# A recurrence on one Trainium2 core: the weights stand in TensorE and the state passes, instead of the other way round

## The chip, the cores and the metric

The kernel is one program on one core of one Trainium2 chip. TensorE (PE in the profile, its loads of the standing operand PEld) multiplies; VectorE (DVE), ScalarE (ACT) and GpSimd (POOL) work elementwise; SyncE (SP) issues most of the transfers. The engines run side by side and wait for each other with semaphores. A matmul has a standing operand, which is loaded first, and a moving one, which passes through it; its result goes to PSUM (`ps`, 8 banks of 512 f32 in each of 128 partitions). The metric is the time of one execution on the device in microseconds, less is better.

## The reference

The whole is one transformer-like block: a recurrence, a long convolution over its states, a gated scan, a shared MLP and a mixture of 16 experts. The change is in the first part alone:

```python
xw = jnp.einsum('ntd,dh->nth', x, Wx) + b          # x: 8 x 512 x 256

def step(prev_h, xw_t):
    next_h = jnp.tanh(xw_t + prev_h @ Wh)          # prev_h: 8 x 256, Wh: 256 x 256
    return (next_h, next_h)
_, hs = jax.lax.scan(step, h0, jnp.swapaxes(xw, 0, 1))
```

The 512 steps can't be done side by side: each needs the state of the one before, for all 8 sequences. All operands are f32. The convolution behind it needs the kernel K, a sum of exponentials of each channel, and all states.

## The kernel before

Constants: P = 128, B = 8 sequences, D = 256, C = 2 (halves of 128 channels), Q = 32, J = 4, W = 64, G = 8 steps in a group, IT = 32 loop turns of 16 steps (two groups, `bank` 0 and 1). J counts four column positions of TensorE's array (`tile_position=(0, Q * j)`): a matmul with at most 32 standing columns can sit in each, and its result lands in partitions 32j to 32j+31.

The state of a step is standing (128 channels x 8 sequences, twice, for the halves k), the weights `wh` move: for each half and each position j one matmul of 8 x 64 (L521). The result has sequences in partitions and 64 channels along a row, so after tanh (L859, into `zt`, two halves of 32 columns) it has to be turned: VectorE transposes blocks of 32 x 32 (L1139, `turn`) into `hring`, a ring of 16 states in `tok`, from which the next step's matmuls load. In PSUM the four banks 0 to 3 hold the sums, two banks for each group.

While a step's state is on its way through ScalarE and VectorE, TensorE adds the input of the same step of the next group to its PSUM area (`xpart`, L500, 8 matmuls with `xst` standing and `wx` moving) and the bias (L503, 4 matmuls of one row, 1 x 8 standing). In steps 11 to 14 of a turn it also does `kernel_sums` (L490), a piece of the convolution's kernel, whose arguments POOL makes once a turn (L399) and ScalarE turns into exponentials in steps 2 to 9 (L863). POOL copies each finished group of states to `uT` (L420, `keep`), and `s_hist` tells that the ring's half may be written again. VectorE builds `cblk` (L1123) in step 4 and takes the finished piece out of PSUM (L1128, L1130) in step 15; SP stores it to `k_pad`.

SP's queue is in order: the first loads (`first`, `state`, nine small `loads`, among them `rows_to` last), then in each turn an `xst` load for each group (`ahead`, waits for `s_xdone`), and beside it either `x_tok` and `slots_in` (turns 0 to 15), or the convolution's matrices into `ring` (turns 17 to 28), and the store of the piece. ScalarE's four exponentials at the start (L847 to L850) and `lam` (L852) stand ahead of its first tanh and wait for all nine loads. `keep_up` is a matmul of zeros over the whole array; eight of 512 columns stand at the program's start.

## Time and profile before

| | us |
|---|---|
| time of the runs, median of 3 | 1144.24 (1143.5 to 1145.04) |
| the profiled execution, its span | 1136.0 |
| PE busy | 1042.3 (92%) |
| PEld busy | 782.3 (69%) |
| DVE busy | 580.7 (51%) |
| ACT busy | 547.1 (48%) |
| POOL busy | 311.8 (27%) |

```text
span 1136.0 us, 62532 instructions
## 1 busy us (share of the span) xinstructions
PE 1042.3 (92%) x26280; PEld 782.3 (69%) x26280; DVE 580.7 (51%) x1954; ACT 547.1 (48%) x1956; POOL 311.8 (27%) x308
## 2 busy tenths in 40 slices
PE   8899999999999999997798999999998999999994
PEld 5566666666666666666685444457888999999994
DVE  2333333333333333336585898998754655645641
ACT  2333333333333333337685777673344665665652
POOL 2111111111011111012240005437602455455455
PEclk7999999999999999999899999999999999999998
DMA  2121221122433333203861001104325566566644
GB/s 86 50 75 63 74 75 63 60 74 66 47 42 41 42 41 44 28 10 58 184 133 41 1 0 62 46 32 145 141 66 177 127 148 156 124 148 149 131 61 47
DMA packets 85349, 89.63 MB, mean 79 GB/s; under 512 B 8657, under 2 KB 71654, under 8 KB 85298
## 3 DMA queue, kind: packets, MB, share of 16 engines
q1 hardware_dynamic: 70706, 71.87, 25.2%
q0 software_dynamic: 14592, 17.10, 9.0%
q8 instruction: 31, 0.51, 0.2%
q14 instruction: 20, 0.16, 0.1%
HBM read 56.82 MB, written 33.96 MB: 80 GB/s over the span
## 4 chain that ended last, share of the span: by engine, by line
PE 64%; DVE 11%; ACT 9%; issue 7%; POOL 5%; DMA 2%; SPq 1%; POOLq 1%; DVEq 0%; ACTq 0%
PE ps L521 18%; PE ps L793 14%; PE ps L807 7%; DVE tok L1139 7%; PE ps L659 7%; ACT zt L859 6%; PE ps L500 4%; PE ps L503 3%; PE ps L709 2%; PE ps L490 2%; POOL slots_in L446 2%; PE ps L581 2%; PE ps L566 2%; PE ps L718 2%; POOL big L420 1%
## 5 line engine op out<-in xcount | busy, mean ns | idle before, releaser
L1139 DVE STREAM_TRANSPOSE tok<-zt 128x32 f32<-128x32 f32 x1024 | 159.6, 194 | 331.3 <-ACT zt L859 310.7
L859 ACT ACTIVATE zt<-ps 128x32 f32<-128x32 f32 x1024 | 146.2, 195 | 332.3 <-PE ps L521 332.3
L521 PE MATMUL ps<-wh,tok 128*8 128x64 f32 x8192 | 212.1, 222 | 43.4 <-DVE tok L1139 1.9
L500 PE MATMUL ps<-wx,xst 128*8 128x64 f32 x8320 | 217.7, 221 | 1.1 <-issue 1.1
L521 PEld LDWEIGHTS ps<-wh,tok 128*8 128x8 f32 x8192 | 118.1, 88 | 123.9 <-DVE tok L1139 110.3
L465 POOL DMA_INDIRECT out<-arena,dest x80 | 127.6, 1595 | 98.8 <-ACT arena L1017 79.6
L503 PE MATMUL ps<-brow,tri 1*8 1x64 f32 x4160 | 153.9, 217 | 0.7 <-issue 0.7
L500 PEld LDWEIGHTS ps<-wx,xst 128*8 128x8 f32 x8320 | 145.0, 91 | 4.7 <-issue 2.4
L793 PE MATMUL ps<-xgT_hi,ew_hi 128*128 128x320 f32 (+1 forms) x384 | 118.7, 309 | 4.1 <-DVE spare L1281 1.6
L793 PE MATMUL ps<-xgT_hi,ew_lo 128*128 128x320 f32 (+1 forms) x384 | 119.0, 310 | 0.0
L793 PE MATMUL ps<-xgT_lo,ew_hi 128*128 128x320 f32 (+1 forms) x384 | 118.2, 308 | 0.0
L1387 DVE TENSOR_TENSOR mid<-mid,ps 128x320 f32<-128x320 f32 (+1 forms) x96 | 46.7, 486 | 106.4 <-ACT mid L1035 104.4
L503 PEld LDWEIGHTS ps<-brow,tri 1*8 1x8 f32 x4160 | 58.2, 82 | 59.9 <-issue 2.9
L420 POOL TENSOR_TENSOR big<-tok,zero 128x128 f32 x64 | 29.1, 455 | 231.8 <-DVE tok L1139 231.8
L399 POOL TENSOR_TENSOR arena<-dta_q,iota_t 128x512 f32<-128x512 f32 x33 | 34.3, 1039 | 208.4 <-PE ps L490 207.3
L659 PE MATMUL ps<-mid,gw 128*128 128x512 f32 x192 | 85.3, 602 | 2.4 <-ACT mid L945 1.6
L446 POOL DMA_INDIRECT slots_in<-tok,arena x64 | 75.5, 1179 | 23.6 <-issue 17.1
L1035 ACT ACTIVATE mid<-ps 128x320 f32<-128x320 f32 (+1 forms) x96 | 41.9, 436 | 72.2 <-PE ps L793 72.2
L793 PEld LDWEIGHTS ps<-xgT_hi,ew_hi 128*128 128x128 f32 (+1 forms) x384 | 68.7, 179 | 4.9 <-DVE spare L1281 1.9
L807 PE MATMUL ps<-ew_hi,eact_hi 128*128 128x256 f32 (+1 forms) x240 | 71.7, 299 | 0.3 <-ACT arena L1017 0.3
L659 PEld LDWEIGHTS ps<-mid,gw 128*128 128x128 f32 x192 | 36.7, 194 | 47.4 <-issue 46.1
L793 PEld LDWEIGHTS ps<-xgT_lo,ew_hi 128*128 128x128 f32 (+1 forms) x384 | 68.8, 179 | 0.0
(206 smaller groups left out, 1754.6 us busy)
## 6 DMA issues: line engine op xcount, KB each, us to landing
ring<-k_pad SPq DMA_DIRECT2D x64, 256.0 KB, 6.2
slots_in<-mid SPq DMA_DIRECT2D x16, 645.0 KB, 3.3
mid<-slots_in SPq DMA_DIRECT2D x16, 645.0 KB, 4.2
arena<-in_ex_down SPq DMA_DIRECT2D x16, 384.0 KB, 3.2
arena<-in_ex_gate SPq DMA_DIRECT2D x16, 352.0 KB, 4.7
arena<-in_ex_up SPq DMA_DIRECT2D x16, 352.0 KB, 5.9
xst<-in_x_steps SPq DMA_DIRECT2D x66, 64.0 KB, 1.8
xtok<-in_x_tok SPq DMA_DIRECT2D x16, 256.0 KB, 2.7
```

Of the source, the lines that this page charges most:

```text
L446: pool.indirect_dma_start(out=slots_in[:, :], out_offset=bass.IndirectOffsetOnAxis(ap=idx[:, k, r:r + 1], axis=0), in_=hid_tok[:, r, :], i ...
L465: pool.indirect_dma_start(out=out[:, :], out_offset=bass.IndirectOffsetOnAxis(ap=dest[:, z, t:t + 1], axis=0), in_=yo[:, z, t], in_offset= ...
L500: nc.tensor.matmul(sums_at(bank, t)[Q * j:Q * j + B], xst[:, bank, k, t], wx[:, k, j * W:(j + 1) * W], start=t < 2 and k == 0, stop=False, ...
L503: last = nc.tensor.matmul(sums_at(bank, t)[Q * j:Q * j + B], tri[0:1, 1, 0:B], brow[:, j * W:(j + 1) * W], start=False, stop=False, skip_g ...
L521: last = nc.tensor.matmul(sums_at(bank, t)[Q * j:Q * j + B], hring[:, (n - 1) % (2 * G), k, 0:B], wh[:, k, j * W:(j + 1) * W], start=False ...
L659: last = nc.tensor.matmul(ps[:, gate_bank(n % NT, q), :], gw[:, q, c, z * P:(z + 1) * P], x1T[:, c, 4 * b:4 * b + 4, :].rearrange("p r t - ...
L793: last = nc.tensor.matmul(ps[0:fw, 2 * h + m % 2, 0:HALF], of(w)[:, c, f0:f0 + fw], v[:, c, hf * HALF:(hf + 1) * HALF], start=c == 0 and p ...
L807: last = nc.tensor.matmul(ps[:, 4 + (z + t) % 2, 0:D], a[0:fw, f, t * P:(t + 1) * P], down_of(w)[0:fw, f], start=f == 0 and p == 0, stop=f ...
L859: nc.scalar.activation(zt[:, n % 2, half], sums_at(n // G, n % G)[:, half], ACT.Tanh).then_inc(s_zt, 1)
L1035: nc.scalar.activation(esil[0:fw, m % 2], ps[0:fw, m % 2, 0:HALF], ACT.Silu).then_inc(s_esil, 1)
L1139: nc.vector.transpose(hring[:, n, k], zt[:, n % 2, k * Q:(k + 1) * Q]).then_inc(s_h, 1)
L1387: nc.vector.tensor_tensor(eprod[0:fw, m % 2], esil[0:fw, m % 2], ps[0:fw, 2 + m % 2, 0:HALF], ALU.mult).then_inc(s_eact, 1)
```

## The change

- `wh` is standing now (128 x 32 columns, L531 of the new file) and the state moves (8 columns). A step has 16 matmuls: for each half o of the result and each half k of the state one for each position j. The result has channels in partitions and sequences along the row, as the next step wants it, so ScalarE writes tanh (128 x 8, L875) straight into `hring`; `zt`, `s_zt` and VectorE's `turn` are gone. `hring` has 8 columns for a state's half instead of 32.
- Half 0 and half 1 of the result lie in different banks (`sums_at(bank, t, o)`), half 0 is complete after 8 of the 16 matmuls (`s_sum[0]`), half 1 after 16. There is a semaphore of its own for each half, on both sides. The wait for `s_hist` moves from VectorE to ScalarE.
- The input is no longer added step by step: `inputs_summed` does it for 8 steps at once, 64 columns moving. A group takes six calls, in its steps t = 1 to 6: for each half o the bias (`brow` standing, one row of 32 columns, and a row of ones moving), then the two halves of `wx`. 24 matmuls a group in place of 96.
- In all steps but 11 to 14 `keep_up(256)` stands behind the rest.
- The nine small loads move from SP's to ScalarE's queue, ahead of its table load; `tri` goes from the first loads to the late ones.
- VectorE's loop holds `kernel_states` and `kernel_out` alone.

On TensorE, in the loop before, from the second wait of step 0 to the start of step 1 (`tok` is the ring of states, `wh` and `wx` the weights, `xst` the inputs):

```order
L521 MATMUL ps<-wh,tok 8x64 [waits s_h]
L521 MATMUL ps<-wh,tok 8x64 x3
L525 ISA
L500 MATMUL ps<-wx,xst 8x64 [waits s_xs1]
L500 MATMUL ps<-wx,xst 8x64 x7
L503 MATMUL ps<-brow,tri 8x64 x4
```

On TensorE, in the loop now, from the end of step 1 to the end of step 2 (`spare` holds the ones, `zero` the zeros of keep_up):

```order
L510 MATMUL ps<-spare,brow 32x64 x4
L489 MATMUL ps<-zero 128x256
L529 REGISTER_ALU
L531 MATMUL ps<-tok,wh 32x8 [waits s_h0]
L531 MATMUL ps<-tok,wh 32x8 x3
L531 MATMUL ps<-tok,wh 32x8 [waits s_h1]
L531 MATMUL ps<-tok,wh 32x8 x11
L535 REGISTER_ALU
L510 MATMUL ps<-xst,wx 32x64 [waits s_xs1]
L510 MATMUL ps<-xst,wx 32x64 x3
```

Eight products a step became 16 with other operands standing, twelve of them behind the second wait, and the 12 products of input and bias became 4 in six steps of eight, with keep_up behind.

On ScalarE, from the program's start to the first step, before:

```order
L845 ACT_TABLE_LOAD
L847 ACTIVATE a_bc<-a_bc 128x64 [waits s_const]
L848 ACTIVATE a_q<-a_q 128x2
L849 ACTIVATE dt_bc<-dt_bc 128x256
L850 ACTIVATE dt_q<-dt_q 128x66
L852 ACTIVATE lam<-dta_q 128x128 [waits s_dta]
L866 UNCONDITIONAL_BRANCH
L866 ISA
L859 ACTIVATE zt<-ps 128x32 [waits s_sum]
L859 ACTIVATE zt<-ps 128x32
```

And now, from the last but one of its nine loads:

```order
L859 DMA iota_t<-in_iota_t 128x128
L859 DMA rows_to<-in_rows_to 128x37
L860 ACT_TABLE_LOAD
L862 ACTIVATE a_bc<-a_bc 128x64 [waits s_const]
L863 ACTIVATE a_q<-a_q 128x2
L864 ACTIVATE dt_bc<-dt_bc 128x256
L865 ACTIVATE dt_q<-dt_q 128x66
L867 ACTIVATE lam<-dta_q 128x128 [waits s_dta]
L882 UNCONDITIONAL_BRANCH
L882 ISA
L874 ISA [waits s_hist]
L875 ACTIVATE tok<-ps 128x8 [waits s_sum0]
```

The nine loads stand ahead of the table load, and a tanh waits for its half alone.

The diff, cut to its core:

```diff
...
         xst = sb("xst", [P, 2, C, G, B])
-        zt = sb("zt", [P, 2, W])
+        ones = spare[0:1, 0:G * B]
         shared = ExitStack()
...
         tok = shared.enter_context(nc.sbuf_tensor("tok", [P, R * DX], F32))
         u_tok = tok[:, 0:R * D].rearrange("p (g j r) -> p g j r", j=J, r=R)
         hid_tok = tok[:, :].rearrange("p (r d) -> p r d", d=DX)
-        hring = tok[:, 7168:7168 + 2 * G * C * Q].rearrange("p (n k q) -> p n k q", n=2 * G, k=C)
+        hring = tok[:, 7168:7168 + 2 * G * C * B].rearrange("p (n k b) -> p n k b", n=2 * G, k=C)
         mid = shared.enter_context(nc.sbuf_tensor("mid", [P, R * D], F32))
         x1T = mid[:, :].rearrange("p (c r t) -> p c r t", c=C, t=P)
         blank = mid[:, 0:CT * DX].rearrange("p (t d) -> p t d", t=CT)
...
         s_kst = sem("s_kst")
         s_state = sem("s_state")
         s_late = sem("s_late")
+        s_sum = [sem("s_sum0"), sem("s_sum1")]
+        s_h = [sem("s_h0"), sem("s_h1")]
         s_tile = [sem("s_tile%d" % n) for n in range(NSLOT)]
         s_yst = [sem("s_yst0"), sem("s_yst1")]
         s_ewg = [sem("s_ewg0"), sem("s_ewg1")]
...
         s_xg = [sem("s_xg0"), sem("s_xg1")]
         block = ctx.enter_context(nc.Block())
-        first = ((wx, wx_d), (tri, tri_d), (brow, b_rec_d))
+        first = ((wx, wx_d), (brow, b_rec_d))
         state = ((wh, wh_d), (h0r, h0_rec))
         loads = ((a_q, a_q_d), (dt_q, dt_q_d), (a_bc, a_bc_d),
                  (dt_bc, dt_bc_d), (c_q, c_q_d), (d_k, d_k_d), (consts, consts_d), (iota_t, iota_t_d), (rows_to, rows_to_d))
-        late = ((ident, ident_d), (h0g, h0_gate), (gw, gate_w), (gb, gate_b), (rw, router_w), (rb, router_b),
+        late = ((ident, ident_d), (tri, tri_d), (h0g, h0_gate), (gw, gate_w), (gb, gate_b), (rw, router_w), (rb, router_b),
                 (resets, resets_d), (iota_e, iota_e_d))
         FIRST_LOADED, STATE_LOADED, LOADED, LATE = 16 * len(first), 16 * len(state), 16 * len(loads), 16 * len(late)
         NT = 2 * C
+        NIN = C * (C + 1)
         def gate_bank(t, q):
             return (2 * t) % 6 + q if q < 2 else 2 + t
...
                 return ((0, 1), (4, 5), (4, 5))[nf % 3]
             return nf % 2, 2 + nf % 2
-        def sums_at(group, t):
-
-            return ps[:, 2 * group + t % 2, t // 2 * W:(t // 2 + 1) * W]
+        def sums_at(bank, t, o):
+
+            return ps[:, 2 * bank + o, B * t:B * t + B]
+
+        def columns(j, o):
+
+            return slice(W * j + Q * o, W * j + Q * o + Q)
         def u_out(engine, copy, half, done):
...
             for dst, src in state:
                 sp.dma_start(dst[:], src).then_inc(s_state, 16)
             sp.dma_start(xst[:, 1], x_steps[1]).then_inc(s_xs[1], 16)
-            for dst, src in loads:
-                sp.dma_start(dst[:], src).then_inc(s_const, 16)
             sp.wait_ge(s_zero, 1)
             sp.dma_start(k_pad[:, 0:P].rearrange("(c p) t -> p c t", p=P), zero[:, 0:C * P].rearrange("p (c t) -> p c t", c=C)).then_inc(s_kst, 16)
...
             def keep(i, half):
-                group = hring[:, G * half:G * half + G, :, 0:B][:, ::-1].rearrange("p t k b -> p k t b")
+                group = hring[:, G * half:G * half + G][:, ::-1].rearrange("p t k b -> p k t b")
                 pool.wait_ge(s_zero, 1)
-                pool.wait_ge(s_h, 4 * G * i + 2 * G * half + 2 * G + 2)
+                pool.wait_ge(s_h[0], 2 * G * i + G * half + G + 1)
+                pool.wait_ge(s_h[1], 2 * G * i + G * half + G + 1)
                 pool.tensor_tensor(uT[:, :, bass.ds(i * (-2 * G) + (S - G - G * half), G), :], group, zeros, ALU.add).then_inc(s_hist, 1)
             with pool.Fori(0, IT) as i:
                 keep(i, 0)
...
                     last.then_inc(s_kmm, 1)
-            def xpart(bank, t):
-
-                for k in range(C):
-                    for j in range(J):
-                        nc.tensor.matmul(sums_at(bank, t)[Q * j:Q * j + B], xst[:, bank, k, t], wx[:, k, j * W:(j + 1) * W],
-                                         start=t < 2 and k == 0, stop=False, skip_group_check=True, tile_position=(0, Q * j))
+            def inputs_summed(bank, n):
+
+                o, c = n // (C + 1), n % (C + 1) - 1
                 for j in range(J):
-                    last = nc.tensor.matmul(sums_at(bank, t)[Q * j:Q * j + B], tri[0:1, 1, 0:B], brow[:, j * W:(j + 1) * W],
-                                            start=False, stop=False, skip_group_check=True, tile_position=(0, Q * j))
+                    if c < 0:
+                        w, v = brow[0:1, columns(j, o)], ones
+                    else:
+                        w, v = wx[:, c, columns(j, o)], xst[:, bank, c].rearrange("p t b -> p (t b)")
+                    last = nc.tensor.matmul(ps[Q * j:Q * j + Q, 2 * bank + o, 0:G * B], w, v, start=c < 0, stop=c == C - 1,
+                                            skip_group_check=True, tile_position=(0, Q * j))
                 return last
+
             for _ in range(WARM):
                 keep_up(512)
             pe.wait_ge(s_ps0, 1)
             pe.wait_ge(s_first, FIRST_LOADED)
             pe.wait_ge(s_xs[0], 16)
-            for t in range(G):
-                last = xpart(0, t)
+            for n in range(NIN):
+                last = inputs_summed(0, n)
             last.then_inc(s_xdone, 1)
             def steps(i, bank):
                 for t in range(G):
                     n = bank * G + t
-                    for k in range(C):
-                        pe.wait_ge(s_h, 4 * G * i + 2 * n + k + 1)
-                        for j in range(J):
-                            last = nc.tensor.matmul(sums_at(bank, t)[Q * j:Q * j + B], hring[:, (n - 1) % (2 * G), k, 0:B], wh[:, k, j * W:(j + 1) * W],
-                                                    start=False, stop=True, skip_group_check=True, tile_position=(0, Q * j))
-                    last.then_inc(s_sum, 1)
-                    if t == 0:
+                    for o in range(C):
+                        for k in range(C):
+                            if o == 0:
+                                pe.wait_ge(s_h[k], 2 * G * i + n + 1)
+                            for j in range(J):
+                                last = nc.tensor.matmul(sums_at(bank, t, o)[Q * j:Q * j + Q], wh[:, k, columns(j, o)], hring[:, (n - 1) % (2 * G), k],
+                                                        start=False, stop=k == C - 1, skip_group_check=True, tile_position=(0, Q * j))
+                        last.then_inc(s_sum[o], 1)
+                    if t == 2:
                         pe.wait_ge(s_xs[1 - bank], 16 * i + 16 + 16 * bank)
-                    last = xpart(1 - bank, t)
-                    if t == G - 1:
-                        last.then_inc(s_xdone, 1)
+                    if 1 <= t <= NIN:
+                        last = inputs_summed(1 - bank, t - 1)
+                        if t == NIN:
+                            last.then_inc(s_xdone, 1)
+                    if not 11 <= n < 11 + 2 * NH:
+                        keep_up(256)
                     if 11 <= n < 11 + 2 * NH:
                         if n == 11:
                             pe.wait_ge(s_ps0, 1)
...
         @block.scalar
         def _(act):
+            for dst, src in loads:
+                act.dma_start(dst[:], src).then_inc(s_const, 16)
             act.preload_act_table(ACT.Tanh)
             act.wait_ge(s_const, LOADED)
             nc.scalar.activation(a_bc[:], a_bc[:], ACT.Exp).then_inc(s_dtm, 1)
...
             def steps(i):
                 for n in range(2 * G):
-                    act.wait_ge(s_sum, 2 * G * i + n + 1)
-                    for k in range(C):
-                        half = slice(k * Q, (k + 1) * Q)
-                        nc.scalar.activation(zt[:, n % 2, half], sums_at(n // G, n % G)[:, half], ACT.Tanh).then_inc(s_zt, 1)
+                    if n % G == 0:
+                        act.wait_ge(s_hist, 2 * i + n // G + 1)
+                    for o in range(C):
+                        act.wait_ge(s_sum[o], 2 * G * i + n + 1)
+                        nc.scalar.activation(hring[:, n, o], sums_at(n // G, n % G, o), ACT.Tanh).then_inc(s_h[o], 1)
                     if 2 <= n < 2 + KG * NH:
                         if n == 2:
                             act.wait_ge(s_kq, i + 1)
...
                 chain[0] = chain[0] + 1
                 dve.wait_ge(s_c, chain[0])
+            nc.vector.memset(ones, 1.0)
             nc.vector.memset(ps[:, 0:5], 0.0).then_inc(s_ps0, 1)
             nc.vector.memset(xc[:], 0.0).then_inc(s_hist, 2)
             nc.vector.memset(ctmp, 0.0).then_inc(s_x1, 2)
+
             dve.wait_ge(s_state, STATE_LOADED)
-            nc.vector.tensor_copy(hring[:, 2 * G - 1, :, 0:B], h0r[:]).then_inc(s_h, 2)
+            for k in range(C):
+                nc.vector.tensor_copy(hring[:, 2 * G - 1, k], h0r[:, k]).then_inc(s_h[k], 1)
             dve.wait_ge(s_const, LOADED)
             dve.wait_ge(s_dtm, 4)
             nc.vector.tensor_tensor(dta_q[:], dt_q[:].unsqueeze(2).to_broadcast([P, NG + KG, NH]), a_q[:].unsqueeze(1).to_broadcast([P, NG + KG, NH]), ALU.mult).then_inc(s_dta, 1)
...
-            def turn(i, n):
-                if n % G == 0:
-                    dve.wait_ge(s_hist, 2 * i + n // G + 1)
-                for k in range(C):
-                    dve.wait_ge(s_zt, 4 * G * i + 2 * n + k + 1)
-                    nc.vector.transpose(hring[:, n, k], zt[:, n % 2, k * Q:(k + 1) * Q]).then_inc(s_h, 1)
-            def steps(i):
-                for n in range(2 * G):
-                    turn(i, n)
-                    if n == 4:
-                        kernel_states(i)
-                    if n == 15:
-                        kernel_out(i)
             with dve.Fori(0, IT) as i:
-                steps(i)
+                kernel_states(i)
+                kernel_out(i)
             u_out(dve, lambda to, v: nc.vector.tensor_copy(to, v), 0, s_uev)
```

## Rows read from the trace of the kernel before

**Rows 1.** Timeline, ScalarE's first and last tanh: start us, length us, engine, line.

```profile
11.97 0.27 ACT L859 ACTIVATE zt<-ps 128x32 f32<-128x32 f32 x2
...
515.40 0.29 ACT L859 ACTIVATE zt<-ps 128x32 f32<-128x32 f32 x2 [0.69 <-PE ps L521]
```

**Rows 2.** The page's costliest groups: busy us, mean ns | idle before, releaser.

```profile
L1139 DVE STREAM_TRANSPOSE tok<-zt 128x32 f32<-128x32 f32 x1024 | 159.6, 194 | 331.3 <-ACT zt L859 310.7
L859 ACT ACTIVATE zt<-ps 128x32 f32<-128x32 f32 x1024 | 146.2, 195 | 332.3 <-PE ps L521 332.3
...
L521 PEld LDWEIGHTS ps<-wh,tok 128*8 128x8 f32 x8192 | 118.1, 88 | 123.9 <-DVE tok L1139 110.3
```

**Rows 3.** Timeline of one steady step.

```profile
300.70 0.41 PE L521 MATMUL ps<-wh,tok 128*8 128x64 f32 x16
...
300.93 0.41 PE L500 MATMUL ps<-wx,xst 128*8 128x64 f32 x16
301.18 0.28 ACT L859 ACTIVATE zt<-ps 128x32 f32<-128x32 f32 x2 [0.49 <-PE ps L521]
...
301.26 0.29 PE L503 MATMUL ps<-brow,tri 1*8 1x64 f32 x8
...
301.41 0.31 DVE L1139 STREAM_TRANSPOSE tok<-zt 128x32 f32<-128x32 f32 x2 [0.66 <-ACT zt L859]
...
301.67 0.41 PE L521 MATMUL ps<-wh,tok 128*8 128x64 f32 x16
```

**Rows 4.** Timeline of TensorE in the convolution: 32 columns standing.

```profile
554.22 0.30 PE L569 MATMUL ps<-arena 128*32 128x64 f32 x8
554.33 0.41 PE L566 MATMUL ps<-ring,arena 128*32 128x128 f32 x8
```

**Rows 5.** Groups by form, loads of 32 columns: 553 to 556, then 547.9 to 551.4.

```profile
L569 PEld LDWEIGHTS ps<-arena 128*32 128x32 f32 x32 | 1.0, 110 | 0.0
...
L569 PEld LDWEIGHTS ps<-arena 128*32 128x32 f32 x32 | 1.6, 177 | 0.1
```

**Rows 6.** Timeline of TensorE where the array's division changes.

```profile
5.90 0.29 PE L503 MATMUL ps<-brow,tri 1*8 1x64 f32 x8
6.12 0.41 PE L500 MATMUL ps<-wx,xst 128*8 128x64 f32 x16
...
538.85 0.66 PE L590 MATMUL ps<-ident,arena 128*128 128x128 f32 x4
539.43 0.42 PE L566 MATMUL ps<-ring,arena 128*32 128x128 f32 x8
```

**Rows 7.** Timeline of the start.

```profile
0.74 1.28 ACT L845 ACT_TABLE_LOAD   x1 [0.74 <-PEq L1497]
...
7.65 1.44 SPq L294 DMA_DIRECT2D rows_to<-in_rows_to  x1
...
10.52 0.26 ACT L847 ACTIVATE a_bc<-a_bc 128x64 f32<-128x64 f32 x1 [8.50 <-DMA rows_to<-in_rows_to]
```

**Rows 8.** The page's transfers: number, KB each, us to landing.

```profile
ring<-k_pad SPq DMA_DIRECT2D x64, 256.0 KB, 6.2
```

**Rows 9.** Windows: from:to, us, busy of PE, PEld, DVE, ACT, POOL, granted clock, DMA, GB/s.

```profile
8.64:12.05 3.41, 1.93 (x84) 1.10 (x72) 0.29 (x1) 1.10 (x7) 0.43 (x2) 1.00 0.20 49
18.88:22.29 3.41, 3.41 (x112) 2.16 (x107) 0.93 (x6) 1.05 (x7) 0.00 (x0) 0.50 0.02 5
100.00:500.00 400.00, 365.67 (x16856) 242.81 (x16856) 138.72 (x898) 137.28 (x924) 48.52 (x77) 1.00 0.26 52
541.11:544.53 3.42, 1.06 (x38) 0.80 (x30) 2.20 (x8) 1.98 (x4) 1.24 (x1) 1.00 0.83 181
544.53:547.94 3.41, 2.53 (x29) 2.00 (x30) 0.00 (x0) 0.58 (x3) 0.71 (x1) 0.50 0.91 194
```

**Rows 10.** Timeline of one step at half the clock.

```profile
17.07 0.61 PE L521 MATMUL ps<-wh,tok 128*8 128x64 f32 x16
...
17.46 0.65 PE L500 MATMUL ps<-wx,xst 128*8 128x64 f32 x16
17.75 0.29 ACT L859 ACTIVATE zt<-ps 128x32 f32<-128x32 f32 x2 [1.53 <-PE ps L521]
...
18.04 0.40 PE L503 MATMUL ps<-brow,tri 1*8 1x64 f32 x8
```

4 lines of the change are left out of this document (2 added, 2 removed).

## The prediction

> [...]
>
> (1) *The price p of such a set.* The trace has no product with 8 columns moving. Upper bound: products with 32 columns standing and 64 moving go at 0.11 us per 8, so 0.056 per set [rows 4], and fewer moving columns can't take longer. Lower bound: a load. One of 32 columns shows 110 ns [rows 5], one of 8 columns 88 in the same clock [rows 2]: 22 ns for 24 columns, 0.9 ns each, so 32 columns occupy a position for 28 ns or so, and the next load for that position can't begin before the product ahead has taken up its weights. With 64 columns moving that hides; with 8 (an eighth of the 53 ns that 0.057 leaves after some issue, 7 ns) it is the load that counts. I take p = 0.030, nearest to the load row, and keep 0.028 to 0.057.
>
> (2) *The chain of one step.* Half 0 is summed first, but half 0 of the next step needs both halves of the state too, so the chain goes through half 1: its tanh, then the 6 sets from the second wait on. First to last product: first load 0.027, five sets of 0.030, 0.02 of stagger: 0.197. From the last product to tanh: today 0.48 less the 0.194 from first to last start is 0.286, less 0.047 for 56 columns fewer: 0.24. Tanh to TensorE: 0.23 today from tanh to a waiting engine, of which 0.195 is the instruction; 24 columns fewer may save 0.01; the hop into TensorE is 0.05, where the hop into VectorE is 0.03: 0.235. Sum **0.67 us** a step against 0.97. The transposes, 0.26 a step, are gone, and nothing replaces them.
>
> (3) *TensorE's own time in a step.* Here the cover is thin. The one-row bias product and keep_up(256) use another division of the array than the sums. What a change of division costs is in the trace: 16 instructions before the one-row product take 0.33 instead of 4 x 0.057 [rows 3], and 8 one-row instructions take 0.22 instead of 0.11 until the next can start [rows 6]; four whole-array products of 128 columns (0.107 each at 2.4 GHz, 0.43, and about 0.05 for the first load) are followed only 0.58 after the first start [rows 6]. So 0.10 to 0.11 each. Whole-array work of 256 bf16 columns streams 0.107 at 2.4 GHz, with 0.015 for its load (bounds 0 and 0.055).
> - Steps without input (4 of 16): sums 0.267 (0.027 + 8 x 0.03), change 0.105, keep_up 0.122, change 0.105: 0.60, under the chain's 0.67.
> - Steps with a wx set pair (0.114): 0.71. Five of 16.
> - Steps with a bias pair: one change more, 0.82. Three of 16.
> - Steps with kernel_sums in place of keep_up (4 of 16): three 0.67 by the chain; the one with a bias 0.73.
>
> Sum for 16 steps: 7 x 0.67 + 5 x 0.71 + 3 x 0.82 + 0.73 = 11.43, 0.714 a step. 511 of them are 365 us; a loop turn costs 0.07 more than its steps today (0.985 against 0.97, mostly), 2 us in all.
>
> (4) *Loads on ScalarE's queue.* rows_to is issued at 7.65 and the first activation stands at 10.52, tanh at 11.97 [rows 7]. Nine issues of 0.48 from 0.74 put rows_to at 4.6, and the table load of 1.28, now behind them, still ends by 7.5. Gain 3 us; nothing if the first activation waits for another transfer. TensorE has 12 sets of input to do instead of 80 before the first step; it is hidden either way.
>
> (5) *What hides.* A ring load takes 5.7 to 6.2 us to land [rows 8] and two go in each loop turn, now 11.5 us long, not 15.6; xst has 12 steps (8.6 us) between its release and its use. POOL's copy and arguments (0.46 and 1.04 us) have half a turn, 5.7 us. VectorE keeps three small operations per turn. All at nothing; if an xst load came late behind the ring, up to 2 us in each of 12 turns, 24 us, which is in the range.
>
> (6) *The clock.* It is at 1.2 GHz from 12.05 to 25.7 today, after TensorE stood still before 12.45 (1.93 of 3.41 us busy) [rows 9]. After the change TensorE stands still from about 6.3 to 9, so I expect a slow start here too, of about the same 13 us, at 0.2 to 0.4 us a step: 3 to 6 us, 3 taken.
>
> Sum: 503.4 - 365 - 2 - 3 + 3 = 136 us less. Span 1000, time **1008 us**.
>
> **Where a rule speaks against it.** Sixteen products start within 0.23 us, 14 ns apart [rows 3], because the four positions run side by side. The Trainium skill, "TensorE: Matmul & The Clock Gate", Part 1, "Wait — 56ns, not 53.3ns?", says that start to start never drops below about 25 ns however small the product; the row disagrees for products in different positions, and an estimate by that rule (32 x 0.025 a step, plus 0.45 of the rest) would be 1.25 us a step, slower than today. The measurement decides.
>
> **The rivals.**
> *A. A small product costs as much as one of 64 columns* (p = 0.057, the upper bound of (1)). The chain becomes 0.81, sums 0.483, the kinds of step 0.82, 0.93, 1.03, 0.81 and 0.95; mean 0.90; 460 us. Saved 43 - 2 + 3 - 3 = 41: **1103 us**. For it: no row shows less than 0.056 per set. Against: what fills that set is its 64 columns. Beside it: the Trainium skill, "TensorEngine Tiling (Array Packing)", "Instruction Overhead", says that a product of one column has the latency of one with 60; by that rule it is this rival. Chance 0.12.
>
> *B. Half clock throughout, loads lengthened with it: slower.* The place is the same stage. At 1.2 GHz a load of 32 columns shows 177 ns, not 110 [rows 5]: p = 0.057. The step before shows the rest of the prices at that clock [rows 10]: sets of 64 columns 0.10 to 0.107 (0.39 for the first four), a change of division 0.15 (0.58 for 16 instructions less four sets), first product to tanh 0.68, of which 0.30 lies between the first and the last start. Chain 0.38 - 0.09 (56 columns fewer) + 0.33 (six sets) + 0.24 = 0.86; sums 0.48 + change 0.15 + keep_up 0.23 + change 0.15 = 1.02; with a wx pair 1.23; with a bias 1.38; kernel steps 0.91 and 1.24. Mean 1.146, 586 us, with the loop turns and the loads of (3) and (4) 82 more than now: **1226 us**. keep_up itself does harm there, since TensorE is then the bound in every step. It decides from p = 0.037 on at that clock (at p = 0.030 the mean is 0.93). For it: the start will be at low clock, and a step in which products stream 8 columns works the array less; the clock fell again at 544.53, behind a stretch with 1.06 of 3.42 us busy [rows 9]. Against: today's low stretch ended while steps with waits ran, and it held 400 us on end at full clock with ten sets of 0.057 and some 0.1 of changing in each 0.97 [rows 9, 3]. Chance 0.16.
>
> *C. Half clock throughout, loads not lengthened* (p = 0.030): chain 0.72, kinds 0.80, 1.01, 1.16, 0.72, 1.02; mean 0.932; 476 us: **1116 us**. Chance 0.10.
>
> *D. The clock changes to and fro.* Half of the steps as in the forecast, half as in B: **1117 us**, with 1060 to 1170 for other shares. Chance 0.10.
>
> *E. It doesn't bind as said*: the changes of division overlap with the waiting, every step runs on the chain, 0.66: 337 us, **980 us**. Chance 0.02 beyond the forecast's own range.
>
> **How the numbers follow.** The forecast has 0.50, with its own range 975 to 1045 (p up to 0.04, late xst loads). The range over the cases: from 975 up over A, C and most of D, to 1150, which leaves out B with 0.16, the top of D and a little below. Faster (by over 0.2%, 2.3 us, what a measurement can tell from no change): forecast, A, C, E and most of D, 0.82. Within: 0.02, a share of D. Slower: B, 0.16.
>
> **What would show it.** In the profile after: the sets of products with 8 columns, start to start, 0.03 (0.057 is A or B); tanh start to tanh start 0.67 in steps without input, 0.71 and 0.82 with it; the granted clock 1.0 behind the first 30 us (0.5 is B or C); ScalarE's idle time ended by TensorE; VectorE's transposes gone; tanh first at 9. Wrong it would be if the last wait in a step were on VectorE, POOL or a transfer, or if the stages behind the recurrence changed their length.

## The result, and the profile after

| | before | after |
|---|---|---|
| time of the runs, median, us | 1144.2 (1143.5 to 1145.04) | 1024.26 (1021.14 to 1031.44) |
| ratio | | 0.897 (0.893 to 0.900) |
| span of the profiled execution, us | 1136.0 | 1019.6 |
| first tanh, last pair of tanh, us | 11.97, 515.40 | 8.99, 392.17 |
| behind the last pair, us | 620.6 | 627.4 |

By the medians the change is worth 120 us. Between the two profiled executions it is 116.4: the recurrence takes 120.2 us less and begins 3.0 earlier, and what stands behind it takes 6.8 more. The ratios below are to the kernel before, which ran beside each group of experiments with medians of 1139.56 us (the extra sets, 32 columns, no zeros), 1143.32 (bias, zeros at the start, the nine loads), 1142.24 (no change of division, both halves) and 1146.83 (the last two). A difference in us between kernels of different groups is therefore uncertain by some us; the lengths of the steps decide. The page's costliest groups of the kernel after (they answer to [rows 2]; columns: busy us, mean ns of one | idle before, releaser):

```profile
L875 ACT ACTIVATE tok<-ps 128x8 f32<-128x8 f32 x1024 | 172.8, 178 | 184.8 <-PE ps L531 184.2
L531 PE MATMUL ps<-tok,wh 128*32 128x8 f32 x16384 | 250.4, 181 | 2.3 <-ACT tok L875 2.1
L531 PEld LDWEIGHTS ps<-tok,wh 128*32 128x32 f32 x16384 | 203.4, 112 | 62.3 <-ACT tok L875 11.8
L1147 DVE TENSOR_SCALAR arena<-ps 128x127 f32<-128x127 f32 x32 | 9.3, 290 | 348.0 <-PE ps L496 348.0
```

The transposes are gone, VectorE waits for the whole recurrence, and ScalarE's idle time is ended by TensorE alone. TensorE is shown busy for 365.82 of the 365.83 us in which its clock is at full (window below), which tells nothing: the steps are of three lengths. ScalarE's timeline of the kernel after (start us, length us; a row holds both halves' tanh, from the first's start to the second's end):

```profile
303.48 0.34 ACT L875 ACTIVATE tok<-ps 128x8 f32<-128x8 f32 x2 [0.40 <-PE ps L531]
304.18 0.34 ACT L875 ACTIVATE tok<-ps 128x8 f32<-128x8 f32 x2 [0.37 <-PE ps L531]
304.89 0.34 ACT L875 ACTIVATE tok<-ps 128x8 f32<-128x8 f32 x2 [0.37 <-PE ps L531]
305.72 0.34 ACT L875 ACTIVATE tok<-ps 128x8 f32<-128x8 f32 x2 [0.49 <-PE ps L531]
306.46 0.34 ACT L875 ACTIVATE tok<-ps 128x8 f32<-128x8 f32 x2 [0.40 <-PE ps L531]
```

Start to start: 0.70 and 0.71 without input products, 0.83 with a bias pair, 0.74 with a `wx` pair. Over all steps at full clock the medians are 0.706, 0.83 and 0.740, and one step of `kernel_sums` with a bias pair 0.708. TensorE's rows of the same place answer to [rows 3]:

```profile
303.71 0.53 PE L531 MATMUL ps<-tok,wh 128*32 128x8 f32 x32
304.18 0.28 PE L489 MATMUL ps<-zero 128*128 128x256 bf16 x1
304.42 0.53 PE L531 MATMUL ps<-tok,wh 128*32 128x8 f32 x32
304.88 0.31 PE L510 MATMUL ps<-spare,brow 1*32 1x64 f32 x8
305.13 0.28 PE L489 MATMUL ps<-zero 128*128 128x256 bf16 x1
```

In the first step TensorE starts the state's products at 303.71, tanh of half 0 follows at 304.18 (0.47) and the next step's first product at 304.42 (0.24), in place of 0.48, 0.23 and 0.26. By the records of single instructions the sets start 0.0315 apart (0.057 before). In the same records, where the sets follow at this pace, each load starts 2 ns behind the start of the product ahead in its position, and its own product 29 ns behind the load's start.

The clock, from windows (from:to, us, busy of PE, PEld, DVE, ACT, POOL, granted clock, DMA share, GB/s):

```profile
9.40:26.47 17.07, 16.91 (x668) 12.40 (x659) 0.93 (x3) 6.51 (x37) 6.06 (x6) 0.50 0.18 63
26.47:392.30 365.83, 365.82 (x19663) 277.00 (x19655) 28.87 (x92) 191.79 (x1113) 57.79 (x92) 1.00 0.33 70
412.20:419.00 6.80, 6.04 (x105) 5.07 (x105) 2.29 (x8) 2.48 (x7) 2.02 (x2) 0.50 0.94 204
494.10:500.90 6.80, 5.68 (x13) 3.22 (x14) 0.32 (x1) 1.19 (x2) 0.00 (x0) 0.50 0.49 166
```

ScalarE's group in the first of these windows:

```profile
L875 ACT ACTIVATE tok<-ps 128x8 f32<-128x8 f32 x33 | 5.9, 178 | 10.7 <-PE ps L531 10.2
```

The first 17 us of the steps run at 1.2 GHz: 33 tanh, 16.5 steps, 1.03 each. Then the clock stays at 2.4 GHz to the end of the recurrence. The last two windows are stretches behind the recurrence where it fell again.

The timeline of the start, ScalarE and its queue, answers to [rows 7]:

```profile
4.56 0.47 ACTq L859 DMA_DIRECT2D rows_to<-in_rows_to  x1
5.06 1.28 ACT L860 ACT_TABLE_LOAD   x1 [5.06 <-issue]
7.50 0.26 ACT L862 ACTIVATE a_bc<-a_bc 128x64 f32<-128x64 f32 x1 [1.16 <-DMA rows_to<-in_rows_to]
8.99 0.24 ACT L875 ACTIVATE tok<-ps 128x8 f32<-128x8 f32 x2
```

### The profile page after: what moved, and what is told of

Read it like the earlier page. It is cut to its first block, busy times and chain, and to the rows that moved or that the text cites. A ratio compares the mean times of both kernels' runs of the same rounds, so it can differ in the third digit from the quotient of the medians.

```text
span 1019.6 us, 58437 instructions
## 1 busy us (share of the span) xinstructions
PE 967.6 (95%) x25496; PEld 769.3 (75%) x25496; DVE 437.3 (43%) x932; ACT 574.5 (56%) x1956; POOL 309.5 (30%) x308
## 4 chain that ended last, share of the span: by engine, by line
PE 80%; issue 5%; DVE 4%; POOL 4%; ACT 3%; DMA 3%; ACTq 0%; POOLq 0%; SPq 0%; DVEq 0%
PE ps L531 21%; PE ps L806 15%; PE ps L489 8%; PE ps L820 8%; PE ps L672 8%; PE ps L510 7%; PE ps L722 3%; POOL slots_in L452 2%; PE ps L594 2%; PE ps L579 2%; PE ps L496 2%; PE ps L731 2%; DMA slots_in<-tok,arena 1%; PE ps L582 1%; PE ps L749 1%
## 5 line engine op out<-in xcount | busy, mean ns | idle before, releaser
L875 ACT ACTIVATE tok<-ps 128x8 f32<-128x8 f32 x1024 | 172.8, 178 | 184.8 <-PE ps L531 184.2
L531 PE MATMUL ps<-tok,wh 128*32 128x8 f32 x16384 | 250.4, 181 | 2.3 <-ACT tok L875 2.1
L531 PEld LDWEIGHTS ps<-tok,wh 128*32 128x32 f32 x16384 | 203.4, 112 | 62.3 <-ACT tok L875 11.8
L1147 DVE TENSOR_SCALAR arena<-ps 128x127 f32<-128x127 f32 x32 | 9.3, 290 | 348.0 <-PE ps L496 348.0
L489 PE MATMUL ps<-zero 128*128 128x256 bf16 (+1 forms) x392 | 113.6, 293 | 1.3 <-POOL zero L399 1.3
L510 PE MATMUL ps<-xst,wx 128*32 128x64 f32 x2080 | 83.0, 227 | 0.0
L452 POOL DMA_INDIRECT slots_in<-tok,arena x64 | 73.4, 1147 | 23.6 <-issue 17.1
L806 PEld LDWEIGHTS ps<-xgT_hi,ew_lo 128*128 128x128 f32 (+1 forms) x384 | 68.6, 179 | 0.0
L820 PE MATMUL ps<-ew_hi,eact_lo 128*128 128x256 f32 (+1 forms) x240 | 67.8, 282 | 0.0
```

The costliest lines, as they stand in the source:

```text
L452: pool.indirect_dma_start(out=slots_in[:, :], out_offset=bass.IndirectOffsetOnAxis(ap=idx[:, k, r:r + 1], axis=0), in_=hid_tok[:, r, :], i ...
L489: nc.tensor.matmul(ps[:, 6, 0:columns], zero16[:, 0:P], zero16[:, 0:columns], start=True, stop=True)
L510: last = nc.tensor.matmul(ps[Q * j:Q * j + Q, 2 * bank + o, 0:G * B], w, v, start=c < 0, stop=c == C - 1, skip_group_check=True, tile_posi ...
L531: last = nc.tensor.matmul(sums_at(bank, t, o)[Q * j:Q * j + Q], wh[:, k, columns(j, o)], hring[:, (n - 1) % (2 * G), k], start=False, stop ...
L806: last = nc.tensor.matmul(ps[0:fw, 2 * h + m % 2, 0:HALF], of(w)[:, c, f0:f0 + fw], v[:, c, hf * HALF:(hf + 1) * HALF], start=c == 0 and p ...
L820: last = nc.tensor.matmul(ps[:, 4 + (z + t) % 2, 0:D], a[0:fw, f, t * P:(t + 1) * P], down_of(w)[0:fw, f], start=f == 0 and p == 0, stop=f ...
```

## The experiments

Twelve kernels ran. The question was, first, why the chain of a step is 0.706 and not 0.67; second, what TensorE's own time in a step is made of; third, what decides the clock, since the rivals lived on it. The rate of steps can be read from one row for each kernel: the number of tanh between 100 and 300 us, two for a step. For the kernel after it is 542, 0.738 a step:

```profile
L875 ACT ACTIVATE tok<-ps 128x8 f32<-128x8 f32 x542 | 91.4, 178 | 95.6 <-PE ps L531 95.6
```

### A set more in half 1, or in half 0

```diff
+                            if o == 1 and k == 1:      # o == 0 in the other
+                                for j in range(J):
+                                    nc.tensor.matmul(sums_at(bank, t, o)[Q * j:Q * j + Q], zero16[:, 0:Q], zero16[:, 0:B],
+                                                     start=False, stop=False, ..., tile_position=(0, Q * j))
```

Half 1, expected:

> The changed kernel with one set more in every step: four products of zeros (bf16, 32 loaded columns, 8 moving) into half 1, ahead of its products with the second half of the state; zeros are added, so nothing computed changes. Theory S (ScalarE sets the distance: in a step without input work the tanh of half 1 starts 0.159 us behind the tanh of half 0 and not when its sums are there; 0.706 = 0.229 + 0.075 + 0.243 + 0.159): a set of 0.032 us that only half 1 waits for is hidden in the 0.033 us by which its sums are early: steps without input stay at 0.706, only the 8 of 16 in which TensorE is the bound (0.740 and 0.83) get 0.032 longer, in all +8 us. Theory L (the last product is followed by its tanh after 0.276 us, whatever the place): every step 0.032 longer, +16 us, steps without input at 0.738.

Measured: 1043.86 us. ScalarE's timeline, two steps with `kernel_sums`:

```profile
302.79 0.37 ACT L879 ACTIVATE tok<-ps 128x8 f32<-128x8 f32 x2 [0.44 <-PE ps L535]
303.52 0.37 ACT L879 ACTIVATE tok<-ps 128x8 f32<-128x8 f32 x2 [0.37 <-PE ps L535]
304.26 0.37 ACT L879 ACTIVATE tok<-ps 128x8 f32<-128x8 f32 x2 [0.37 <-PE ps L535]
```

Its group, 516 tanh in 200 us:

```profile
L879 ACT ACTIVATE tok<-ps 128x8 f32<-128x8 f32 x516 | 91.7, 178 | 95.5 <-PE ps L535 91.7
```

Steps without input are 0.738 (0.73 and 0.74 in the rows), 0.032 more, and the pair's row is 0.37 long, not 0.34: half 1's tanh follows 0.192 behind half 0's, not 0.159. Theory S falls. ScalarE doesn't hold the second tanh back; it comes when TensorE's results for half 1 are there. A set in half 1 costs the chain its full 0.032. The total is 20 us above the kernel after (0.918 of before, from 0.913 to 0.923); its slow stretch at the start is also longer here (to 45.5 us, not 26.5).

Half 0, expected:

> The same four products of zeros, but into half 0, behind the wait for the second half of the state. Theory S: half 0's tanh comes 0.032 us later and half 1's with it: every step 0.032 longer, 0.738 in steps without input, +16 us. Theory L: the same, +16 us: only the pair of this run and the one with the set in half 1 tells them apart (S: 16 against 8; L: 16 against 16).

Measured: 1176.97 us, and the pair could not be compared as planned, for TensorE's clock was at half through the whole recurrence (window of the whole stretch, columns as above):

```profile
9.00:550.00 541.00, 539.11 (x22330) 398.35 (x22332) 29.50 (x93) 207.21 (x1148) 63.64 (x97) 0.50 0.23 49
```

ScalarE's group from 100 to 300 us:

```profile
L879 ACT ACTIVATE tok<-ps 128x8 f32<-128x8 f32 x380 | 67.5, 178 | 123.2 <-PE ps L535 116.4
```

380 tanh in 200 us are 1.053 a step. Three of the four executions of this kernel took 1174 to 1181 us and one 1073. The clock records agree with the times: a mean granted clock of 0.759 over the 1172 us of the profiled one means some 565 us at half, and 0.913 in the short one some 190 us (estimates: twice the missing share, times the span). So the same program can spend its recurrence at either level or change over on the way. This is what rivals B to D described, and at half clock it is slower than the kernel before (1139.56 beside it). The medians by kind of step are 0.90 without input, 1.15 with a `wx` pair and 1.27 with a bias pair.

### 32 moving columns in place of 8

```diff
-            return ps[:, 2 * bank + o, B * t:B * t + B]
+            return ps[:, 2 * bank + o, WIDE * t:WIDE * t + B]          # WIDE = 32
-                    last = nc.tensor.matmul(sums_at(...)[Q * j:Q * j + Q], wh[...], hring[:, (n - 1) % (2 * G), k],
+                    last = nc.tensor.matmul(ps[Q * j:Q * j + Q, 2 * bank + o, WIDE * t:WIDE * t + WIDE]..., wh[...],
+                                            hring[:, (n - 1) % (2 * G), k].unsqueeze(1).to_broadcast([P, WIDE // B, B]),
```

> The changed kernel with 32 moving columns in place of 8 in the state's products (each state column four times, the step's sums in every 32nd column of the bank, the other columns filled and never read). Theory P (the start of a set goes by its loads, 0.032 us, and moving columns only add their own stream): sets stay 0.032 to 0.036, the last product to its tanh 0.243 and 10 ns at most, steps without input 0.71 to 0.73, in all +2 to +15 us. Theory M (a set's price goes with its moving columns, from 0.032 at 8 to 0.057 at 64 on a straight line: 0.043 at 32): 8 sets a step cost 0.09 us more, TensorE bounds every step at about 0.76 to 0.92, in all +35 to +45 us.

Measured: 1031.14 us, 0.904 (0.900 to 0.908) of before, 7 us above the kernel after. ScalarE's timeline:

```profile
302.80 0.34 ACT L876 ACTIVATE tok<-ps 128x8 f32<-128x8 f32 x2 [0.39 <-PE ps L532]
303.52 0.34 ACT L876 ACTIVATE tok<-ps 128x8 f32<-128x8 f32 x2 [0.39 <-PE ps L532]
304.25 0.34 ACT L876 ACTIVATE tok<-ps 128x8 f32<-128x8 f32 x2 [0.39 <-PE ps L532]
```

Theory P holds. Steps without input are 0.724, 0.018 more; the sets still start 0.0315 apart; and half 0's last product stands 0.263 before its tanh in place of 0.243. So 24 columns add 0.020 to the time from the last product to tanh and nothing to the pace. From 8 to 64 columns that is 0.047, which with 0.243 gives 0.290; before the change it was 0.286. The pace is that of something else than the columns, as the prediction's part (1) has it, and the records of the loads, with the next product 29 ns behind the start of its load, point at the load. No run here changed the loaded columns alone.

### No zeros between the steps

```diff
-                    if not 11 <= n < 11 + 2 * NH:
-                        keep_up(256)
```

> The changed kernel without the 256 moving columns of zeros per step (12 of 16 steps). Theory D (its two changes of division, 0.108 and 0.212 us from product to product, are what puts TensorE on the path in steps with input products; the clock stays): bias steps fall from 0.83 to about 0.76 or less, wx steps to 0.706, in all -12 to -17 us. Theory K (without them TensorE falls to half clock for the recurrence: steps as in the slow stretch at the start less the zeros, 0.85 to 1.0): +60 to +120 us.

Measured: 1075.87 us (1059.76 to 1080.63), 0.936 (0.927 to 0.946) of before; theory K in direction, with 52 us where it gave 60 to 120. ScalarE's group from 100 to 300 us:

```profile
L873 ACT ACTIVATE tok<-ps 128x8 f32<-128x8 f32 x470 | 83.5, 178 | 105.0 <-PE ps L531 96.6
```

Two rows of its timeline, and behind them the window of the whole recurrence:

```profile
299.99 0.39 ACT L873 ACTIVATE tok<-ps 128x8 f32<-128x8 f32 x2 [0.22 <-PE ps L531]
300.43 0.62 PE L531 MATMUL ps<-tok,wh 128*32 128x8 f32 x32
```
```profile
9.00:446.00 437.00, 424.20 (x19928) 372.52 (x19920) 29.83 (x95) 207.42 (x1150) 63.72 (x98) 1.00 0.28 61
```

0.851 a step. This profile must be read with care. The window shows a clock of 1.00, but the trace has no record of the clock before 450 us, and everything has the lengths of the half-clock stretch of the kernel after, which its timeline shows like this:

```profile
12.63 0.62 PE L531 MATMUL ps<-tok,wh 128*32 128x8 f32 x32
13.18 0.44 PE L510 MATMUL ps<-spare,brow 1*32 1x64 f32 x8
13.55 0.39 PE L489 MATMUL ps<-zero 128*128 128x256 bf16 x1
13.87 0.62 PE L531 MATMUL ps<-tok,wh 128*32 128x8 f32 x32
```

The 32 products' row is 0.62 long, not 0.53, and the tanh pair's 0.39, not 0.34. From these rows I take it that TensorE ran at 1.2 GHz throughout. Two other executions of this kernel bear it out by their granted clock: 0.776 over 1078.7 us is some 480 us at half, and 0.823 over 1057.9 us (the shortest one) some 375, and 40 us at half stand behind the recurrence in the profiled one. So without the zeros the clock was down for most of the recurrence or all of it, and in the kernel after they are needed to keep it up. They are not always enough: the kernel with one set more in half 0 had them too. They have two sides: at full clock they allow 0.740 a step, and at half clock they cost (0.851 without them, 1.03 to 1.05 with them in the slow stretches of the kernel after and of the one with zeros at the start; the rows above have a bias step of 13.87 - 12.63 = 1.24).

### The bias on ScalarE; zeros in the sums' division

```diff
-                    if c < 0:
-                        w, v = brow[0:1, columns(j, o)], ones
...
-        nc.scalar.activation(hring[:, n, o], sums_at(n // G, n % G, o), ACT.Tanh)
+        nc.scalar.activation(hring[:, n, o], sums_at(n // G, n % G, o), ACT.Tanh, bias=brow[:, o:o + 1])
```

> The changed kernel with the bias as ScalarE's own operand of the tanh in place of the one-row products; the input products stand in steps 2 to 5 of each 8. By the steps of the changed kernel's trace (0.706 without input, 0.740 with a pair of input products, 0.83 with a bias pair), if a bias pair's two changes of division are the whole of its 0.124: 11 steps at 0.706 and 5 at 0.740 of 16, mean 0.717 against 0.740, 12 us less, about 1012 against 1024, if the clock stays up as there. Rival 1: the tanh with a bias operand takes longer, and the steps without input get longer than 0.706. Rival 2: with less work in TensorE the clock is at half for the whole recurrence (steps 0.87 to 1.13, as in that state's rows: 0.873 without input, 1.126 with): 80 to 130 us more.

The second kernel has this and also replaces `keep_up(256)`:

```diff
+            def keep_tiled(columns):
+                for j in range(J):
+                    nc.tensor.matmul(ps[Q * j:Q * j + Q, 6, 0:columns], zero16[:, 0:Q], zero16[:, 0:columns], ..., tile_position=(0, Q * j))
```

> As the kernel with the bias as operand, and the 256 columns of zeros now go as four bf16 products of 32 loaded columns, one per column position, so that no step has a change of division. Theory D (the two changes, 0.108 and 0.212 from product to product, are what puts TensorE on the path in steps with input products): all steps 0.706, mean 0.706, 17 us less than the changed kernel, about 1007. Rival: a change costs nothing of its own and the zeros' 0.28 us is what counts: steps with input stay at 0.74. Rival of the clock: half for the whole recurrence: without changes of division a step there is 0.81 to 0.90, +50 us and more.

Measured: 1052.54 and 1052.25 us, both 0.919 (0.916 to 0.922) of before and 28 us above the kernel after. ScalarE's group from 100 to 300 us of the first:

```profile
L871 ACT ACTIVATE tok<-ps,brow 128x8 f32<-128x8 f32 x504 | 107.6, 264 | 80.8 <-PE ps L527 80.8
```

And of the second:

```profile
L875 ACT ACTIVATE tok<-ps,brow 128x8 f32<-128x8 f32 x504 | 107.6, 264 | 80.5 <-PE ps L531 80.5
```

Rival 1: the tanh takes 264 ns, not 178, and from half 1's tanh to TensorE's load it is 0.311 in place of 0.229. All 16 steps of a turn are 0.795, with and without input, in both kernels. (The Trainium skill, "ScalarE: Activation LUTs", "What ACT_TABLE_LOAD costs", says that a pointer operand adds some 93 ns to an activation; the rows show 86.) A chain 0.089 longer costs more than the bias products did on TensorE, and once the chain is 0.795 the changes of division that the second kernel removes are worth nothing, since TensorE has the time for them.

### Zeros at the start

```diff
             last.then_inc(s_xdone, 1)
+            for _ in range(4):
+                keep_up(512)
```

> The changed kernel with four more products of 512 columns of zeros between the first inputs and the first step, where TensorE stands still for 2.3 us and behind which its clock is at half from 9.4 to 26.5 us. If that pause is what lets the clock fall: no or a shorter slow stretch (steps of 1.05 in place of 0.74 for 17 us: 5 us less), 1016 to 1020. If the slow stretch comes of the steps themselves: unchanged, 1021 to 1027, the stretch at the same place.

Measured: 1036.3 us (1026.71 to 1049.81), 0.900 (0.895 to 0.905) of before, no gain. The steps at full clock are the same, but in the profiled execution the slow stretch lasted to 61 us (by the lengths of rows; the clock has no record before 61.5 here). Its group from 30 to 50 us has 38 tanh in 20 us, 1.05 a step:

```profile
L877 ACT ACTIVATE tok<-ps 128x8 f32<-128x8 f32 x38 | 6.8, 178 | 12.0 <-PE ps L533 11.3
```

The zeros did fill the place of the pause, from 6.75 to the first step's products at 8.57:

```profile
6.75 1.89 PE L489 MATMUL ps<-zero 128*128 128x512 bf16 x4
```

But they run at half clock themselves, 0.43 from one product of 512 columns to the next, and the input products ahead of them have the half-clock lengths too (their second row of 16 takes 0.66, in the kernel after 0.43). In this execution the clock was down before the place of the pause, and filling it didn't bring the clock up. So a slow start doesn't need the pause; whether the pause lets a clock fall that is up, as it was in the kernel after, this execution can't tell. When the slow stretch ends differs between executions and kernels (26.5, 45.5, 61 us), at 0.3 us a step, and most of the spread of the times (1021 to 1031 for the kernel after) can come of it. Why it ends when it does is open.

### The nine loads alone

The kernel before with `loads` on ScalarE's queue, nothing else:

> The kernel before with one part of the change alone: the nine small loads issued on ScalarE's queue and not on SyncE's. The first tanh at 9 to 10 us in place of 11.97 and 2 to 3 us less in all (0.998 of before), if nothing else waits; nothing if the first tanh waits for TensorE's first sums or if the clock's slow stretch grows in its place.

Measured: 1142.26 us, 0.998 (0.9954 to 1.0005) of before: and the interval takes in no change. Its timeline, ScalarE at the start and at the last pair:

```profile
8.63 0.26 ACT L847 ACTIVATE a_bc<-a_bc 128x64 f32<-128x64 f32 x1 [2.28 <-DMA rows_to<-in_rows_to]
10.09 0.27 ACT L859 ACTIVATE zt<-ps 128x32 f32<-128x32 f32 x2
514.48 0.29 ACT L859 ACTIVATE zt<-ps 128x32 f32<-128x32 f32 x2 [0.69 <-PE ps L519]
```

The first tanh comes 1.9 us earlier and the last 0.9 earlier. Behind the last pair stand 626.0 us in this execution (span 1140.5), with the kernel before in all its stages.

### No change of division, the tanh as it is

```diff
-        brow = sb("brow", [1, D])
+        brow = sb("brow", [P, D])                 # b in row 0, 127 rows of zeros; ones in 128 rows
-                        keep_up(256)
+                        keep_tiled(256)
```

> The changed kernel without any change of division inside a step, the tanh as it is: the bias row padded with 127 rows of zeros, so that its products load 128 rows and 32 columns like the others, and the 256 columns of zeros as four bf16 products of 32 loaded columns. Theory (a step is the longer of the chain, 0.706, and TensorE's own time, which the changes of division lengthen to 0.740 and 0.83): all steps at 0.706, mean 0.706 against 0.740, 17 us less than the changed kernel, about 1005 if the clock comes up as early as there. Rival 1: the input products themselves fill TensorE (steps with input stay at 0.74, no-input ones at 0.706): 9 us less. Rival 2, of the clock: its level is half for most of the recurrence, as with one set more in half 0: steps 0.85 to 0.90, +50 us or more.

Measured: 1005.85 us, 0.879 (0.876 to 0.883) of before. ScalarE's timeline:

```profile
301.37 0.34 ACT L879 ACTIVATE tok<-ps 128x8 f32<-128x8 f32 x2 [0.15 <-PE ps L535]
302.08 0.34 ACT L879 ACTIVATE tok<-ps 128x8 f32<-128x8 f32 x2 [0.17 <-PE ps L535]
302.78 0.34 ACT L879 ACTIVATE tok<-ps 128x8 f32<-128x8 f32 x2 [0.17 <-PE ps L535]
```

The step from 302.08 on follows a bias pair, its neighbours have `wx` pairs. All 16 steps of a turn are 0.704. That answers the second question: the 0.034 to 0.124 by which steps with input were longer are changes of the array's division, with the one-row products and with the whole-array zeros, not the input's products, which are as many as before. Both were taken away in one run, so the share of each isn't told apart here. TensorE now waits for ScalarE in each step.

### Both halves ahead of the second wait

```diff
-                    for o in range(C):
-                        for k in range(C):
-                            if o == 0:
-                                pe.wait_ge(s_h[k], 2 * G * i + n + 1)
+                    for k in range(C):
+                        pe.wait_ge(s_h[k], 2 * G * i + n + 1)
+                        for o in range(C):
+            return (2, 3, 5, 7)[2 * bank + odd] if o else bank      # half 1: banks of its own for odd steps
```

> As the one with the padded row, and the order undone that completes half 0 first: behind the first half of the state come its products into both halves, behind the second half its products into half 0, then half 1. So that no product of half 1 goes to the bank that the tanh of half 1 reads, the odd steps' half 1 has banks of its own, and the input products of half 1 are made for the even and the odd steps apart (9 pairs for 8 steps). Theory R (0.706 = 0.229 tanh to load, 0.075 to half 0's last product, 0.243 to its tanh, 0.159 for the four sets that half 1 still needs, by the results' pace of 0.040 a set): two of these four sets now run ahead of the second wait: 0.706 less 2 x 0.040 = 0.626, or 0.641 if the two tanhs can follow no closer than the 0.094 of the kernel before: 33 to 41 us less than the padded one, about 965 to 975. Rival: TensorE's own time (8 sets at 0.040, a pair of input sets, the zeros and their gaps) takes more than that: 0.68 to 0.74 and nothing gained in steps with input. Rival of the clock: half for the whole, +50 us or more.

Measured: 998.37 us, 0.874 (0.871 to 0.878) of before, 7.5 us less than the one above, where 33 to 41 were expected; the intervals of the two overlap, the steps' lengths tell them apart. ScalarE's timeline across the end of a loop turn:

```profile
215.68 0.27 ACT L886 ACTIVATE tok<-ps 128x8 f32<-128x8 f32 x2 [0.41 <-PE ps L540]
216.36 0.27 ACT L886 ACTIVATE tok<-ps 128x8 f32<-128x8 f32 x2 [0.41 <-PE ps L540]
217.28 0.27 ACT L886 ACTIVATE tok<-ps 128x8 f32<-128x8 f32 x2 [0.65 <-PE ps L540]
217.96 0.18 ACT L886 ACTIVATE tok<-ps 128x8 f32<-128x8 f32 x1 [0.41 <-PE ps L540]
```

Two things: 15 of 16 steps are 0.678, not 0.641, and the one across the turn is 0.92. The pair's row is 0.27 long, so the tanhs are 0.093 apart, as before the change. But now six sets lie between the first wait and half 0's last product: tanh to load 0.228, six sets 0.201, to tanh 0.249, sum 0.678. The chain has moved from half 1 to half 0. The expectation had worked out the path through half 1 alone. The step across the turn is taken up in the next kernel.

### The same, input products early in the group

```diff
-                    if t >= 1:
-                        for item in range(3) if t == 1 else (t + 1,):
+                    if 1 <= t <= 4:
+                        for item in range(3) if t == 1 else (2 * t - 1, 2 * t):
```

> As f3 (0.678 in 15 of 16 steps, 0.923 in the step across the loop's end), but the nine pairs of input products of a group stand in its steps 1 to 4 (three, two, two, two), so that TensorE's last step before the loop's branch holds no input products. If they are what the branch came late behind: the step across the end at 0.68 to 0.72, 6 to 8 us less than f3, about 991. Rival: the branch and the first instructions behind it cost the 0.245 whatever stands ahead (with 0.678 there is less idle time to hide them than with 0.706): unchanged, 998, or more if two pairs and the zeros no longer fit beside the chain.

Measured: **991.68 us**, 0.866 (0.862 to 0.871) of before, the lowest median here, 33 us less than the kernel after. ScalarE's group from 100 to 300 us:

```profile
L886 ACT ACTIVATE tok<-ps 128x8 f32<-128x8 f32 x590 | 79.5, 177 | 106.2 <-PE ps L540 106.2
```

The step across the turn is 0.712, as expected. By the records of TensorE's queue the branch itself takes 0.207 in every kernel. In the kernel after it starts 0.114 ahead of half 0's tanh and costs nothing, here 0.098 ahead and costs 0.034, in the kernel above (f3) 0.032 ahead and costs 0.245: there the first product of the next step starts 0.1 late, and the eight sets are interrupted for another 0.13. Steps with two or three pairs of input products stay at 0.678.

### Half a block less ahead of the second wait

Column positions 2 and 3 of half 1's first block go behind half 0's last block:

```diff
+  for o, k, js in ((0, 0, range(J)), (1, 0, (0, 1)), (0, 1, range(J)), (1, 0, (2, 3)), (1, 1, range(J))):
```

> As f4, and of the two sets of half 1 behind the first wait, column positions 2 and 3 go behind half 0's products with the second half. In f3 TensorE never waits for the second half: 0.228 tanh to load, 0.201 for six sets, 0.249 to the tanh, 0.678. With half a block less ahead: the second wait ends last, tanhs 0.12 apart, 0.12 + 0.228 + 0.074 + 0.243 = 0.665, 7 us less than f4. Rival: products that use two column positions only take as long as four, TensorE's six sets stay six: 0.678 or more, nothing gained or a loss of up to 0.03 a step (15 us).

Measured: 996.17 us (990.07 to 998.19), 0.870 (0.866 to 0.874) of before, not told apart from the one above. Its steps are 0.672, and the pair's row is 0.30 long:

```profile
301.20 0.30 ACT L886 ACTIVATE tok<-ps 128x8 f32<-128x8 f32 x2 [0.37 <-PE ps L540]
```

The path is the one expected: tanhs 0.126 apart, 0.228 to the load, 0.074, 0.243, in sum 0.672 against 0.678. It is 0.126 and not 0.12 since half 1's last product starts four set times behind half 0's, with three sets' worth of products between: two products in two positions take as long as four in four, which is the rival's part. The step across the turn is 0.84 or 0.875, and that takes the gain back. No input product stands ahead of the branch here either, so they aren't all that decides what a turn costs. The branch starts 0.062 to 0.082 ahead of half 0's tanh, later than in the kernel above and earlier than in f3, and the cost lies between theirs. But the kernel with the padded row has turns with the branch 0.048 ahead at no cost, with half 1's tanh further behind half 0's. So the start of the branch doesn't decide alone; what does, and what interrupts the sets behind it, is open.

## Why the prediction came out as it did

Its time was 1008, its range 975 to 1150; it was 1024.26. It forecast faster, by the mechanism that took place.

- **(1) The price of a set** was right: 0.0315 against 0.030, and it doesn't go by the columns (pace unchanged with 32 of them). That it goes by the load fits the records (29 ns from a load's start to its product, 28 estimated), but was not tested by itself. Rival A falls as a price, and C with its 0.030 at half clock: there a set is 0.053. Beside it: the Trainium skill, "TensorEngine Tiling (Array Packing)", "Instruction Overhead", says that a product of one column has the latency of one with 60. The runs disagree: 24 columns add 0.020 from the last product to tanh.
- **(2) The chain** is where the step's time was mis-sized: 0.67 against 0.706. The tanh to TensorE took 0.229 (0.235 predicted), the six sets from the second wait 0.201 (0.197), and half 0's last product to its tanh 0.243 (0.24). The term that failed is this last one for half 1, by which the chain goes: 0.276. Half 1's last product starts 0.126 behind half 0's, but its tanh 0.159 behind. I took one latency for both. That ScalarE keeps the two tanhs apart was refuted. What the 0.033 is stays open: a pace of the results slower than that of the starts would explain it in the kernel after, but with six sets in a row ahead of half 0 it showed 0.249 and not more (half 1, two sets later, again 0.278), in the kernel with the split block it was absent (0.242), and at half clock too (0.268 for both halves).
- **(3) TensorE's own time**: steps with `wx` 0.740 (0.71), with bias 0.83 (0.82). That TensorE is the bound there by its changes of division was right, and the kernel without them has 0.704 in every step. The mean of 16 steps was 0.740 against 0.714: 0.026, of which 0.016 is (2), 0.009 the `wx` steps, 0.002 the bias steps, less 0.001 for the kernel step with a bias. On the some 494 steps at full clock that is 12.7 us. The 0.07 for a loop turn didn't come, 2 us less.
- **(4) The loads**: first tanh 8.99 against 9 predicted, 3.0 us gained at that point. Alone on the kernel before, the same edit moved the first tanh by 1.9 us and the median by an amount within its interval.
- **(5) What hides** did hide: no step's idle time on ScalarE ends by a transfer or POOL, and no step is longer than its kind.
- **(6) The clock**: the slow start was forecast with 13 us costing 3; it was 17 us and cost 16.5 steps of 1.03 less 0.740, 5 us. What followed was full clock to the end, as forecast. B to D had a chance of 0.36, and they were near: with one set more in half 0, or with the zeros taken away, TensorE spent the recurrence of the profiled execution at 1.2 GHz. So the forecast's full clock was in part luck: no row that it had tells how near the other level was. B's price there (1.146 a step, 1226 us) was too high, measured 1.053 with a set more (1174 us). Its set price of 0.057 was right (0.053), but its steps without input have 0.87 in the slow stretch of the kernel after, where it gave 1.02, so the gaps around the zeros were priced too high.
- **Behind the recurrence** the prediction had no change, and named a change of length there as a sign of being wrong. The trace has 6.8 us more, and longer stretches at half clock. The granted clock of the first 104.6 us behind the last pair was 0.93 before; the window of after:

```profile
392.30:496.90 104.60, 83.61 (x2185) 71.94 (x2184) 68.55 (x224) 74.94 (x213) 28.46 (x16) 0.89 0.54 106
```

It isn't the change's doing, as far as the runs tell: the kernel before with the nine loads moved has 626.0 us there, and the last four kernels, which differ from each other only in the recurrence, from 620 to 630. The length goes with the time at half clock in this part: 25 us at half in the execution before and 620.6 in all, 37 and 627.4 after, 25 and 620.0 in the last kernel, 47 and 633.5 in the one with zeros at the start, about 0.5 us for each us at half over the fourteen traces. It is scatter between executions that a sum made on one profiled execution takes in as if it were a constant.
- **Span and time**: the sum added 8.2 us to the span, the distance of one execution's span from the median of others. Each run's own time is 1.9 us above its span; the rest was the profiled execution being a quick one. In the profiled execution the miss is 19.6 us (1019.6 against 1000): 12.7 steps, 2 slow start, less 2 turns, 6.8 behind. On the medians it is 16, since the kernel after was only 4.7 above its span and not 8.2: by luck the number looks 3.5 us better than the sum was.

## What to carry to other kernels

In a chain that crosses engines, write the path down for each half, and for each half its own latency; a step is the longest of these paths and of each engine's own time, and an edit is worth only as much as the path that takes its place allows (0.159 to 0.093 between the tanhs brought 0.026 a step). On TensorE, keep everything between dependent products in one division of the array: a padded bias row and zeros in four column positions, together, took 18 us off where moving the bias to the engine on the chain cost 28. And when filler keeps the clock up, check by the lengths of rows, not by one clock number, at which level the stage ran.

## What the runs showed of the hardware that was not expected

- Products in four column positions with 32 loaded and 8 moving columns start 8 ns apart on average, a set of four in 0.0315 us at full clock and 0.053 at half; with 32 moving columns the pace is the same. Products in two positions only gain nothing over four.
- The level of TensorE's clock in one and the same program can differ between executions for a whole stage: 1073 to 1181 us for one kernel.
- With no zeros between them, the steps kept the half-clock lengths for 437 us, though TensorE's busy time was 424.2 of them.
- A tanh of 128 x 8 takes 178 ns with constants and 264 with a per-partition bias, and 0.082 of these 0.086 us stand in the wait from tanh to the next load (0.311 against 0.229).
- A loop's branch on TensorE takes 0.207 us. Started 0.114 ahead of half 0's tanh it cost nothing, 0.098 ahead 0.034, 0.062 to 0.082 ahead 0.17 to 0.20, and 0.032 ahead 0.245, more than itself; what decides between them is open.
